# An RWKV layer and a gated MLP on one core: load queues, turns of shares and high parts, and the order of work on the engines

## What is computed

```
_layernorm(x)                          # then an RWKV time-mix layer
h = ln1(x); hh = time_shift(h)
k, v, r = (h*m + hh*(1-m)) @ W.T       # for Wk, Wv, Wr, each with its own m
x = x + sigmoid(r) * wkv(k, v) @ Wo.T  # no state: wkv needs this token's k, v only
h = ln2(x); hh = time_shift(h)
kk = (h*m + hh*(1-m)) @ Wkey.T         # 512 -> 2048
kv = silu(kk) @ Wval.T
x = x + sigmoid((...) @ Wcr.T) * kv
# then residual, _layernorm and a gated MLP with 2048 inner features
out = (silu(gate) * up) @ w_down.T
```

## Time and profile before

| | |
|---|---|
| median of 3 runs | 1109.93 us (1108.16 to 1110.4) |
| profiled execution | 1111.04 us, its span 1109.2 us |
| mean granted TensorE clock | 0.989 |
| busy share: TensorE, VectorE, ScalarE, GpSimd | 96%, 58%, 44%, 49% |

### The profile page before, as it was taken

One profiled execution on the slowest core, in us unless ns is written; L12 is line 12 of the kernel. 1 busy time (PEld: TensorE's weight loads), 2 busy tenths in 40 slices (PEclk: granted clock), 3 DMA queues, 4 the chain that ended last, 5 costly groups with the idle time before them and its releaser, 6 DMA issues. The chain is left out here.

```text
span 1109.2 us, 13090 instructions
## 1 busy us (share of the span) xinstructions
PE 1065.0 (96%) x4704; PEld 875.0 (79%) x4704; DVE 641.9 (58%) x1106; ACT 485.7 (44%) x807; POOL 542.1 (49%) x451
## 2 busy tenths in 40 slices
PE   5979999999999999999998999999998999999998
PEld 4758888777788887888786888887876888888887
DVE  7867756685355457465348567676668433333334
ACT  6765676856534435323344433334434222222221
POOL 6483552733766554544435555664554333333322
PEclk9989999999999999999998999999999999999999
DMA  8000222258834444553312466565436454444422
GB/s 306 1 1 1 38 39 76 39 209 255 322 125 150 145 171 122 190 160 109 128 62 105 165 231 192 198 220 190 171 114 218 133 191 141 152 144 150 151 77 76
DMA packets 45233, 157.18 MB, mean 142 GB/s; under 512 B 4080, under 2 KB 4208, under 8 KB 40560
## 3 DMA queue, kind: packets, MB, share of 16 engines
q1 hardware_dynamic: 30000, 108.10, 27.9%
q0 software_dynamic: 15168, 48.24, 14.5%
HBM read 97.60 MB, written 58.72 MB: 141 GB/s over the span
## 5 line engine op out<-in xcount | busy, mean ns | idle before, releaser
L1215 DVE TENSOR_TENSOR resid<-bank,resid 128x512 f32<-128x512 f32 x240 | 164.7, 689 | 244.6 <-PE bank L481 243.0
L490 PE MATMUL bank<-combo,left 128*128 128x512 f32 x672 | 265.1, 395 | 12.7 <-ACT bank L890 7.2
L1447 POOL TENSOR_TENSOR inner<-made,inner 128x512 fp32r<-128x512 f32 x128 | 167.0, 1326 | 220.0 <-ACT inner L845 220.0
L491 PE MATMUL bank<-combo,left 128*128 128x512 f32 x672 | 263.5, 392 | 0.0
L492 PE MATMUL bank<-combo,left 128*128 128x512 f32 x672 | 263.3, 392 | 0.0
L479 PE MATMUL bank<-right,inner 128*128 128x512 f32 x512 | 199.3, 389 | 0.0
L480 PE MATMUL bank<-right,inner 128*128 128x512 f32 x512 | 199.2, 389 | 0.0
L481 PE MATMUL bank<-right,inner 128*128 128x512 f32 x512 | 199.2, 389 | 0.0
L1425 POOL TENSOR_TENSOR left<-quart,left 128x512 fp32r<-128x512 f32 x96 | 116.2, 1232 | 104.8 <-ACT left L810 53.9
L490 PEld LDWEIGHTS bank<-combo,left 128*128 128x128 f32 x672 | 127.3, 190 | 42.7 <-ACT bank L890 8.5
L492 PEld LDWEIGHTS bank<-combo,left 128*128 128x128 f32 x672 | 127.4, 190 | 26.8
(11 more groups left out here) (128 smaller groups left out, 1461.7 us busy)
## 6 DMA issues: line engine op xcount, KB each, us to landing
kept_left<-left SPq DMA_DIRECT2D x24, 1792.0 KB, 8.2
left<-kept_left POOLq DMA_DIRECT2D x24, 1024.0 KB, 7.1
left<-kept_left POOLq DMA_DIRECT2D x24, 768.0 KB, 5.1
tall_staged<-tall SPq DMA_DIRECT2D x64, 256.0 KB, 3.6
quart<-wide SPq DMA_DIRECT2D x24, 512.0 KB, 4.2
raw<-kept SPq DMA_DIRECT2D x32, 256.0 KB, 6.3
landed<-wts SPq DMA_DIRECT2D x20, 256.0 KB, 5.8
resid<-x POOLq DMA_DIRECT2D x4, 1024.0 KB, 9.2
```

Source lines behind the costliest of these rows:

```text
L490: pe.matmul(acc[:], hi, combo[:, c, k, 0, :], start=fresh and k == 0, stop=False, skip_group_check=True)
L491: pe.matmul(acc[:], hi, combo[:, c, k, 1, :], start=False, stop=False, skip_group_check=True)
L1215: dve.tensor_tensor(tile, A[s][:], tile, ALU.add).then_inc(added, 1)
L1447: pool.tensor_tensor(inner[:, h % 4, i, 1, :], made_at(n), inner[:, h % 4, i, 0, :].bitcast(F32), ALU.subtract).then_inc(inner_lo, 1)
```

## The change

- Start: the vectors and the identity are loaded from ScalarE's queue, the four tiles of x stand alone at the head of SP's. ScalarE calls Sigmoid once on a small tile, ahead of everything else. VectorE's first norm has another order, and GpSimd starts on Wr's low parts only when all four tiles are normed.
- All mixes on ScalarE: shares and high parts in turns (share 0, 1, high 0, share 2, high 1, share 3, high 2, high 3).
- Block 1: `receptance_gate(1)` goes ahead of `mixed("k", 1)`; `mix("r", 1)` ahead of `norm1_stats(2)`, and on GpSimd `operand_lo("r", 1)` ahead of `norm1(2)`; Wo's low parts move from GpSimd to VectorE, behind `gated_value(0)`.
- Block 3: `output(3)` ahead of `right_sums(0)`.
- Unit 0: `key_tile(0, 0)` ahead of `unit_right_hi(0)`; `unit_right_lo(0)` behind the second half of `unit_left_lo`.

```diff
@@ sync: start
-            sp.dma_start(resid[:, 0, 0], x_blocks[0][:, 0, :]).then_inc(x_first[0], 16)
-            sp.dma_start(vec[:], vectors).then_inc(vec_loaded, 16)
-            for n in range(1, SUBS):
+            for n in range(SUBS):
                 sp.dma_start(resid[:, 0, n], x_blocks[0][:, n, :]).then_inc(x_first[n], 16)
-            sp.dma_start(ident[:], identity).then_inc(ident_loaded, 16)
@@ scalar: mixes
-                for k in range(KT):
-                    act.wait_ge(transposed, KT * b + k + 1)
...
             def mixed(kind, b):
-                rest_of(kind, b)
-                mix_hi(kind, b)
+
+                rest_of(kind, b, 0)
+                for k in range(1, KT):
+                    rest_of(kind, b, k)
+                    if k == 1:
+                        place_free(kind, b)
+                    operand_hi(kind, b, k - 1)
+                operand_hi(kind, b, KT - 1)
@@ scalar: unit
-                if is_key(u):
+                if is_key(u) and u:
                     unit_right_hi(u)
...
                     key_tile(u, 0, X)
+                    if u == 0:
+                        unit_right_hi(u)
@@ scalar: order
+            act.dma_start(vec[:], vectors).then_inc(vec_loaded, 16)
+            act.dma_start(ident[:], identity).then_inc(ident_loaded, 16)
+            act.wait_ge(half_set, 1)
+            act.activation(table[:], minus_half[:, 0, 0:1], ACT.Sigmoid).then_inc(table_loaded, 1)
             act.wait_ge(vec_loaded, 16)
...
-                mixed("k", b)
-                receptance_gate(b)
+                if b == 1:
+                    receptance_gate(b)
+                    mixed("k", b)
+                else:
+                    mixed("k", b)
+                    receptance_gate(b)
@@ vector: first_norm1 (summed now also does the aggregate and the variance of its tile)
-                summed(0)
-                for s in range(SUBS):
-                    if s + 1 < SUBS:
-                        summed(s + 1)
-                    if s == 1:
-                        constants()
...
-                    if s:
-                        normed(s - 1)
-                normed(SUBS - 1)
+                summed(0)
+                constants()
+                summed(1)
+                summed(2)
+                normed(0)
+                summed(3)
+                for s in range(1, SUBS):
+                    normed(s)
@@ vector: order
             wkv_weight(0)
+            mix("r", 1)
             norm1_stats(2)
             for b in range(2):
                 back_to_first(b)
-            mix("r", 1)
             for b in range(1, BLOCKS):
                 gated_value(b - 1)
+                if b == 1:
+                    matrix_lo(ITEM_O)
                 mix("k", b)
...
             mix_ck(2)
+            output(BLOCKS - 1)
             right_sums(0)
-            output(BLOCKS - 1)
@@ gpsimd: unit
-                if is_key(u):
+                if is_key(u) and u:
                     unit_right_lo(u)
                 if u + 1 in FRESH:
                     unit_left_lo(u + 1, 1)
-                if not is_key(u):
+                if not is_key(u) or u == 0:
                     unit_right_lo(u)
@@ gpsimd: order
             first_norm1()
+            pool.wait_ge(z1_ready, SUBS)
             matrix_lo(ITEM_R, range(KT - 1))
...
             operand_lo("v", 0)
+            operand_lo("r", 1)
             norm1(2)
-            operand_lo("r", 1)
-            matrix_lo(ITEM_O)
```

More of the change, by code:

```diff
@@ L226, in build @@
         minus_half = sb("minus_half", [P, 2, SUBS])
+        table = sb("table", [P, 1])
         TILE = 4 * BT
@@ L323, in build @@
         last_r_lo = sem("last_r_lo")
-        const_done = sem("const_done")
+        const_done, table_loaded = sem("const_done"), sem("table_loaded")
         ln_moments, ln_stats, ln_var = sem("ln_moments"), sem("ln_stats"), sem("ln_var")
@@ L719, in operand_hi, with rest_of @@
                 act.activation(place(kind, b, k, 0), made[:, n % RING, :], ACT.Copy).then_inc(op_hi, 1)
-            def rest_of(kind, b):
+            def rest_of(kind, b, k):
                 n, m = operand_at(kind, b), MIXES[kind]
                 transposed, beta = (t2_psum, 3) if kind == "cr" else (t1_psum, 1)
-                for k in range(KT):
-                    act.wait_ge(transposed, KT * b + k + 1)
[L727 to L731, removed]
+                act.wait_ge(transposed, KT * b + k + 1)
+                if n + k >= RING:
+                    act.wait_ge(op_lo, n + k - RING + 1)
+                    act.wait_ge(op_hi, n + k - RING + 1)
+                act.activation(made_at(n + k)[:, 1:BT], A[k][:, 0:BT - 1], ACT.Identity,
+                               bias=vec[:, beta, k:k + 1], scale=rest_g[:, m, k:k + 1]).then_inc(rest_part, 1)
             def rest_of_ck(b):
@@ L759, in wkv_weight, with place_free @@
                     act.activation(B[j][:], B[j][:], ACT.Exp).then_inc(e2_inv, 1)
-            def mix_hi(kind, b):
+            def place_free(kind, b):
                 if kind == "y" and b == BLOCKS - 1:
@@ L781, in mix_hi @@
                     act.wait_ge(x1_kept[1], 16)
+            def mix_hi(kind, b):
+                place_free(kind, b)
                 for k in range(KT):
```

## The result

The changed kernel took 1118.49 us (median of 4 runs, 1117.24 to 1119.69) against 1109.99 before: ratio 1.008, 95% interval 1.0062 to 1.0097. It is slower, as forecast, but by 8.5 us instead of 2.85, and above the range. The profiled execution took 1117.24, the lowest of the four, with a span of 1115.4.

A forecast was written before the change was run, and what follows sets the result against it. TensorE, busy 96% of the span, was taken as the bound. Key(1)'s +5.65, the output sums' -3.4 and unit 0's +0.6 gave +2.85 us, put onto the median 1109.93: 1112.8 us, range 1103 to 1117.

The forecast's parts named there:

- Start: At the first matmul: earlier x tiles, a new norm order and the high part second gain 2.5 us, bounds 2.0 and 3.0.
- What a mix in turns costs: In ScalarE's and VectorE's mixes: each holds VectorE 1.1 us longer wherever ScalarE waits for VectorE.
- Block 0: Up to value(0): the start's 2.5 us run into VectorE and are gone; value(0) starts 0.8 us later than before.
- the slack of 0.43: At value(0)'s bank: VectorE's margin before TensorE needs it, where the start's gain would end even with no turns.
- Block 1: At receptance(1) and key(1): late VectorE work and low clock cost +5.65 us, bounds +1 and +9.
- Output sums ahead of operand sums: At channel_receptance(1): output(3) starts earlier, the wait falls from 2.1 to 0.8 us; -3.4, bounds -4 and -1.5.
- Unit 0: In unit 0's new order: the first out tile comes 0.6 us later, bounds -1.5 and +2.3.
- upper bounds of +9, +1, -1.5 and +2.3: In us, the worst cases for key(1), blocks 2 and 3 between, output sums ahead of operand sums, and unit 0.
- Rival (a): At key(1): VectorE isn't what it waits for, output(0) hides the chain; faster, -9.1 us to 1101; chance 0.28.
- Rival (b): Same chain, but no low clock in receptance(1) and a cheaper cold start: +0.6 us, 1110.5, about the same; chance 0.26.

The follow-up runs named there:

- Experiment one: The changed kernel with every mix making its four shares first and its four high parts after them, as before: 1113.58 us.
- experiment six: The kernel before with only the start changed (two queues, early sigmoid table, first norm's order, GpSimd's wait for it), no turns, old orders elsewhere: 1108.32 us.
- Experiment eight: The changed kernel with output(0) ahead of norm1_stats(3) on VectorE: 1116.23 us.
- experiment three: The changed kernel with right_sums(0) ahead of output(3) again: 1116.09 us.
- experiment five: The changed kernel with ScalarE's channel_receptance(2) moved ahead of rest_of_ck(3) and combo B21: 1114.93 us.
- experiment seven: The changed kernel with unit 0 in its order of before: 1115.42 us.
- nine: The changed kernel without turns, channel_receptance(2) early, and block 1 reordered on ScalarE, GpSimd and VectorE, with output(0) ahead of norm1_stats(3): 1105.56 us.
- experiment ten: The changed kernel without turns, channel_receptance(2) early, unit 0's old order, output(0) ahead of norm1_stats(3), block 1 reordered with norm1(2) ahead of mix k on VectorE: 1101.15 us.
- two: The changed kernel with receptance_gate(1) behind mixed k of block 1 again: 1111.50 us.
- four: The changed kernel with the old order around mix r of block 1 on VectorE and GpSimd: 1119.26 us.

## Why the prediction was wrong

**Start.** Right in kind, a little short: r(0) at 14.34 instead of 14.96, a gain of 3.1 where 3.0 was the bound. VectorE took up the third x tile at 6.39 instead of 7.13, 0.74 earlier where 0.5 was taken, and no longer waited for it. That isn't where the forecast was short, for the first norm tile began at 7.45 for 7.5. The last twelve transposes took 2.68 where three times 1.1 was taken, and ScalarE's first share began at 11.85 for 12.4. Two queues load at once here, though the vectors' place among the transfers changed too, so the runs don't tell what made the tile earlier by more than the 0.42 of issue. By the rule of the Trainium skill (DMA: Bandwidth & Descriptors, Issuing engines are not separate DMA queues) only the issue time would have been saved; the runs neither bear it out nor refute it. The sigmoid table was loaded at 1.67 and no load lies ahead of receptance_gate(0); a later load at 41.03 is followed by its activation at 42.32, 1.29 behind. The drain that the Trainium skill adds to a load (ScalarE: Activation LUTs, What ACT_TABLE_LOAD costs) doesn't show here either.

**What a mix in turns costs.** Right: mixes of k in block 1 at 72.49, then 74.80, and done 4.3 later (76.78). Experiment one puts the whole of it at 4.9 us of the time, with the 1.6 of clock in it.

**Block 0.** The times were right (mix v at 35.50, the transposes of norm1(1) at 41.40 behind a wait of 1.90, value(0) at 44.49), one reason was not. "The rest of Wk, the statistics of block 1, Wv and norm1(1) follow as they did" holds for the changed kernel only because turns lost 2 us in r and k. My clause that the gain would end "even with no turns" at the slack of 0.43 is refuted by experiment six: without turns VectorE follows the start, and value(0) is 2.6 earlier.

**Block 1.** Right throughout, in its terms and in their sum: receptance(1) 58.31 for 58.3, the low clock behind its wait, the 8.35 for 8.4, the start of key(1) 90.32 for 90.2, the low clock behind that. Experiment eight shows that the chain is a sum of pieces: 2.9 us taken out shortens the wait by 2.95. That a low clock fell into receptance(1) was forecast from two waits that had one behind them; behind the same wait it stayed away in three experiments, so this term came true in the profile and isn't certain.

**Output sums ahead of operand sums: the step that failed.** The gain at channel_receptance(1) came (wait 0.75, no low clock). "T3's high parts and norm2(3) behind them still come in time" came true as well, as far as it goes (TensorE waits 0.06 at norm2(3)). What failed is the term of -3.4, with its bounds of -4 and -1.5, which this sentence was to secure: I had looked at operands only, and put what the later VectorE does to ScalarE at nothing. The banks of channel_receptance(3) wait for sigmoids that ScalarE runs behind the last mix, rest_of_ck(3) and B21. In the kernel before the first of these sigmoids began at 254.72 and channel_receptance(3) at 255.53, so they were 0.2 from being late. With TensorE 3.8 us earlier through the edit the sigmoids would have had to come 3.8 earlier too; they came 1.4 earlier, and the trace shows ScalarE waiting 1.70 there for an operand sum that the edit had put behind the output sums, a wait that experiment three doesn't have. So this step was worth 0, not -3.4 (experiment three). The turns have a share in the 3.07 (without them it is 2.00, experiment one). The order of the sigmoids is what decides: experiment five, which changes nothing else, removes the wait of 3.07 and the low clock behind it (1.6, by the time from channel_receptance(3) to unit 0: 12.54 against 10.90 before) and gives 4.1 us back by unit 0.

**Unit 0.** +0.6 forecast, +0.2 measured against before, but +1.3 against the old order in the changed kernel. Before, the unit had one wait of 2.53 and a stretch at the lower level behind it (a mean of 0.67 from 278.0 to 283.2); in experiment seven the same order has three waits of 1.01, 0.82 and 0.74 and the clock stays at 1.00; the new order has 0.83, 1.77 and 1.20, also at 1.00. Between these two the sum of waits differs by 1.23, which is the 1.3. So the step was sized against a low clock that the old order need not have. With TensorE earlier still the gap between the two orders shrinks to 0.3 (experiments nine and ten).

**The account.** At the first out tile TensorE is 7.6 later than before where 2.85 was forecast: 4.75 of miss, of which +2.5 at norm2(3) holds 0.2 and the stage up to unit 0 all the rest, less 0.4 in unit 0. Behind the out tile 1.4 us come back, since the span is only 6.2 longer (1115.4 less 1109.24). One stretch at the low clock that the kernel before had and the changed one hadn't accounts for about that. The same transposes in the view by stretches, the kernel before:

```profile
551.90:555.10 3.20, 3.20 (x12) 2.72 (x12) 0.00 (x0) 1.91 (x4) 0.00 (x0) 0.50 1.13 392
```

And the changed kernel:

```profile
558.30:561.60 3.30, 3.30 (x23) 3.04 (x24) 0.00 (x0) 1.33 (x3) 0.40 (x1) 1.00 0.95 273
```

From the span's 6.2 to the medians' 8.5 there are 2.3 more: the profiled execution before lay 1.1 above its median, the one after 1.25 below. What the other executions of the changed kernel spent isn't in the trace; a low stretch costs about 1.6, so one or two would do it, but that stays open. The range was too narrow by the prediction's own terms: its upper bounds of +9, +1, -1.5 and +2.3 add up to +10.8, 1120.7 and not 1117. Rival (a) fell, since key(1) waited. Rival (b) fell too: its premise, no low clock in receptance(1), came true in the profiles of experiments two, three and seven, but the output sums' step that it counted on was worth nothing.

## What to carry to other kernels

When an edit makes the bound engine earlier, list for each of its later starts every semaphore it waits for, banks freed by another engine's program order as well as operands, with the slack of each; the smallest slack, not the removed wait, is the gain. On an engine that runs in order, work that frees a bank goes ahead of work that feeds a later stage, and a step that waits for the bound engine's end (here the gates) must not stand ahead of the next stage's preparation. Turns of produce and round help where they are the first thing the bound engine waits for, and cost a hand-off each where the middle engine is late.

## What the runs showed of the hardware

- The same wait is not always followed by a low clock. receptance(1) began behind a wait of 2.6 us in the profiles of the changed kernel and of experiments two to five, seven and eight. A stretch at 0.50 followed in the changed kernel and in four, five and eight, and none in two, three and seven, nor behind one of 2.90 in one. Key(1), where it still waited for the same chain, started at 88.84 and 88.76 in three and seven, and at 90.3 in the changed kernel, four and five: 1.5 us between executions of like work, where the runs of the changed kernel spread over 2.45. It need not last: in seven the low stretch around the start of key(1) was longer (84.7 to 94.9, against 87.1 to 93.9), and norm1(2) was only 0.4 earlier.
- VectorE and GpSimd slow each other in operations from one tile to another. Wo's four low parts on VectorE (59.97) took 6.01 us beside four operations of GpSimd's (59.06) that took 6.37; four GpSimd subtractions of the same form took 5.03, with VectorE idle. norm1(2), four tiles, took 1.90 alone (experiment ten), 3.83 beside GpSimd for part of its length, and 5.55 all beside it. VectorE's mixes, which read a bank, kept their 0.75 beside it (74.80 and 75.98, GpSimd at work from 74.17).
